# Turning the second batch's attention weights and the last normalised tiles by DMA, after splitting them into halves

## The reference

```python
def _layernorm(x, axis=-1, eps=1e-05):
    m = jnp.mean(x, axis=axis, keepdims=True)
    v = jnp.var(x, axis=axis, keepdims=True)
    return (x - m) / jnp.sqrt(v + eps)
...
        Q = jnp.einsum('btx,dx->btd', text, Wq) + bq
        K = jnp.einsum('bpx,dx->bpd', features, Wk) + bk
...
        scores = jnp.einsum('btd,bpd->btp', Q, K) * scale
        attn = jax.nn.softmax(scores, axis=-1)
        attended = jnp.einsum('btp,bpd->btd', attn, features)
...
        gate = _matmul_lora(x, gate_w, gate_a, gate_b)
        up = _matmul_lora(x, up_w, up_a, up_b)
        hidden = jax.nn.silu(gate) * up
        out = _matmul_lora(hidden, down_w, down_a, down_b)
```

## Time and profile before

| | us |
|---|---|
| median of 3 executions | 1181.67 |
| lowest and highest | 1180.48, 1183.46 |
| the profiled execution, its time | 1183.68 |
| the profiled execution, its span | 1181.9 |
| mean granted TensorE clock | 0.991 |

### The profile page before, as it was taken

How to read it: one execution, slowest core, us unless ns; L and a number is a source line. 1 busy time by engine, 2 the same in 40 slices (tenths; PEclk the granted TensorE clock), 3 DMA queues, 4 the chain that set the end, 5 groups by cost and what they waited for, 6 DMA issues and landing times.

```text
span 1181.9 us, 16528 instructions
## 1 busy us (share of the span) xinstructions
PE 1124.5 (95%) x6416; PEld 564.7 (48%) x6422; DVE 787.8 (67%) x1571; ACT 482.3 (41%) x723; POOL 166.0 (14%) x194
## 2 busy tenths in 40 slices
PE   4786999899989999999999999999999999999998
PEld 2353554744445444555444444444444444444444
DVE  8999988889994187977767676676766662222220
ACT  6896753772144224535343443434343341111110
POOL 4883340082004010210000000000000000000000
PEclk9997999999999999999999999999999999999999
DMA  9620000123032034201211212121211421111310
GB/s 370 262 93 1 2 1 1 72 80 100 1 107 86 1 94 157 107 1 38 71 58 50 72 36 72 37 72 36 72 50 30 150 66 48 48 48 49 126 47 18
DMA packets 25919, 83.58 MB, mean 71 GB/s; under 512 B 3633, under 2 KB 4273, under 8 KB 25841
## 3 DMA queue, kind: packets, MB, share of 16 engines
q1 hardware_dynamic: 25840, 82.53, 20.3%
HBM read 76.22 MB, written 6.29 MB: 70 GB/s over the span
## 4 chain that ended last, share of the span: by engine, by line
PE 72%; DVE 19%; ACT 5%; issue 2%; DMA 1%; SPq 0%; ACTq 0%; DVEq 0%
PE PAIR L2380 32%; PE PAIR L2019 11%; PE PAIR L2020 11%; PE PAIR L2021 11%; DVE X L1449 2%; PE PAIR L2337 1%; DVE BST L1247 1%; DVE BST L1248 1%; DVE PAIR L1401 1%; DVE POOL L1275 1%; PE PAIR L2412 1%; DVE LORA L1400 1%; DVE X L1318 1%; DVE LORA L1402 1%; DVE XT L1312 1%
## 5 line engine op out<-in xcount | busy, mean ns | idle before, releaser
L2019 PE MATMUL PAIR<-POOL 128*128 128x512 f16 x672 | 255.8, 381 | 2.4 <-DVE POOL L1492 2.4
L2020 PE MATMUL PAIR<-POOL 128*128 128x512 f16 x672 | 255.6, 380 | 0.0
L2021 PE MATMUL PAIR<-POOL 128*128 128x512 f16 x672 | 255.6, 380 | 0.0
L2380 PE MATMUL PAIR<-XT,POOL 128*128 128x512 f16 x1008 | 228.2, 379 | 0.0
L2380 PEld LDWEIGHTS PAIR<-XT,POOL 128*128 128x128 f16 x1008 | 97.8, 98 | 113.7
L2380 PE MATMUL PAIR<-X,POOL 128*128 128x512 f16 x504 | 115.7, 379 | 0.0
L2021 PEld LDWEIGHTS PAIR<-POOL 128*128 128x128 f16 x672 | 65.8, 98 | 80.3 <-issue 1.4
L2019 PEld LDWEIGHTS PAIR<-POOL 128*128 128x128 f16 x672 | 65.6, 98 | 67.5 <-DVE POOL L1492 4.1
L2020 PEld LDWEIGHTS PAIR<-POOL 128*128 128x128 f16 x672 | 65.7, 98 | 63.8 <-issue 0.6
L1634 DVE SCALAR_TENSOR_TENSOR STG<-STG,PAIR 128x1024 f32<-128x1024 f32 (+2 forms) x32 | 28.3, 884 | 90.0 <-PE PAIR L2412 90.0
L952 ACT ACTIVATE POOL<-STG 128x1024 f16<-128x1024 f32 (+2 forms) x32 | 25.3, 790 | 148.1 <-DVE STG L1634 148.1
(11 more groups left out here) (306 smaller groups left out, 1758.1 us busy)
## 6 DMA issues: line engine op xcount, KB each, us to landing
STG<-in_gate_w SPq DMA_DIRECT2D x21, 512.0 KB, 3.6
STG<-in_up_w SPq DMA_DIRECT2D x21, 512.0 KB, 4.3
STG<-in_ctx_t SPq DMA_DIRECT2D x16, 512.0 KB, 4.0
STG<-in_ctx SPq DMA_DIRECT2D x16, 512.0 KB, 4.3
STG<-in_down_w SPq DMA_DIRECT2D x16, 512.0 KB, 3.5
POOL<-in_ctx SPq DMA_DIRECT2D x12, 512.0 KB, 11.2
X<-in_x SPq DMA_DIRECT2D x8, 512.0 KB, 9.8
out_t<-X SPq DMA_DIRECT2D x16, 256.0 KB, 2.9
```

Of the source, the lines that this page charges most:

```text
L2019: e.matmul(dst, l_hi, r_hi, start=first, stop=False)
L2020: e.matmul(dst, l_hi, r_lo, start=False, stop=False)
L2021: return e.matmul(dst, l_lo, r_hi, start=False, stop=last)
L2380: i = e.matmul(dst, blk[:, a_, k, :], src[:, b_, k, :], start=(opens and k == 0 and n == 0), stop=(k == KD // 2 - 1 and n == 2), skip_grou ...
```

## The change

No transpose of these tiles is left on PE. The float32 value is first split where it lies, in rows, and the two float16 halves are turned by DMA transposes that SP issues.

- Weights of tiles 4 to 7: `weights_hi` and `weights_lo` split Y[1] into TURN[0] (in XT); `turn_weights(g)` issues two DMA transposes of 128x1024 into AT. `attend(g)` waits for them on x_in[g].
- H4[0..3]: split into TURN[1], `turn_fourth(u)` issues two of 128x1024 each.
- The five pieces of each t: `difference(t, p)`, now all 16 on DVE (T2's goes into PSUM), `piece_hi` on ACT and `piece_lo` on DVE, 20 of each, and `turn_piece(t, p)`, two DMA transposes of 128x512 each, 40 in all. Source space is short, so for t = 1 ACT waits ahead of B22 and DVE ahead of the low half of T2 until all ten transposes of t = 0 have landed; `keep_first(j)` waits for those of t = j.
- PE's S1(0) waits for all pieces of t = 0 and 1 and T1 of t = 2 and 3; S2(0), S4(0), S3(0) and A22(0) for T2, B22, T3 and T4 of t = 2 and 3.
- SP's list gets the 56 transposes: those of tiles 4 and 5 between context loads, those of tiles 6 and 7 and of H4[0..3] after the first four weight loads, the 40 pieces after the spill and the next two loads. All stand on the one SP queue.

```diff
+TURNED = 48
+T1, T2, B22, T3, T4 = range(5)
+LANDED = 32
...
+def turn_order(t, p):
+
+    return 5 * t + p if t < 2 else 10 + 2 * p + t - 2
...
+        TURN = [[XT[:, b, :, :, :].rearrange("p s k t -> p (s k t)")[:, 2 * D * t:2 * D * (t + 1)]
+                 .rearrange("p (s n) -> p s n", s=2) for t in range(BT)] for b in range(B)]
...
+        def wait_turned(e, t, p=None):
+
+            if t < 2:
+                e.wait_ge(turn_in(t, p), LANDED + 5 * 32)
+            else:
+                e.wait_ge(turn_in(t, p), LANDED + 2 * 32)
+
+        def difference(e, t, p):
 
             b11, b21, b12, b22 = (H4[g][:, h * HALF:(h + 1) * HALF] for g in (t, BT + t) for h in range(2))
...
+            if p == T1:
+                e.wait_ge(n4_ok, BT + t + 1)
+                e.wait_ge(x4t_lo, t + 1)
+                e.tensor_tensor(b11, b12, b11, ALU.subtract).then_inc(tg_ok, 1)
...
+            def turn_weights(g):
+                t = g % BT
+                e.wait_ge(at_lo, g + 1)
+                e.wait_ge(av_p, t + 1)
+                for s_ in range(2):
+                    e.dma_start_transpose(AT[:, s_, :, t * P:(t + 1) * P], TURN[0][t][:, s_, :]).then_inc(x_in[g], 16)
+
+            def turn_fourth(u):
+                for g in range(BT, NT):
+                    e.wait_ge(x_in[g], TURNED)
+                e.wait_ge(x4t_lo, u + 1)
+                for s_ in range(2):
+                    e.dma_start_transpose(XT[:, 0, s_, :, u * P:(u + 1) * P], TURN[1][u][:, s_, :]).then_inc(x_in[u], 16)
+
+            def turn_piece(t, p):
+                if t == 0 and p == T1:
+                    for u in range(BT):
+                        e.wait_ge(x_in[u], TURNED)
+                    e.wait_ge(spilled, 16 * BT)
+                e.wait_ge(x4t_lo, BT + turn_order(t, p) + 1)
+                e.dma_start_transpose(placed(t, p)[:, 0], high_half(t, p)).then_inc(turn_in(t, p), 16)
+                e.dma_start_transpose(placed(t, p)[:, 1], low_half(t, p)).then_inc(turn_in(t, p), 16)
...
+            def piece_lo(t, p):
+                e.wait_ge(x4t_hi, BT + turn_order(t, p) + 1)
...
+                elif t == 1 and p == T2:
+                    wait_turned(e, 0)
+                e.tensor_tensor(low_half(t, p), value(t, p), high_half(t, p), ALU.subtract).then_inc(x4t_lo, 1)
...
@@ -1913,44 +2009,60 @@
             slab_add(3)
             add_attended(4)
             stats_of(4)
+            norm_ask(4, 5)
             fourth_lo(0)
             fourth_lo(1)
-            attended_terms(4)
+            norm_rest(4, 5)
+            fourth_lo(2)
+            fourth_lo(3)
             block_lo(0, "S3")
             block_lo(0, "A22")
+            add_attended(5)
+            stats_of(5)
+            norm_ask(5, 6)
+            for p in (T1, T2, T3):
+                difference(e, 0, p)
+            norm_rest(5, 6)
+            piece_lo(0, T1)
+            difference(e, 0, T4)
+            for p in (T2, B22, T3, T4):
+                piece_lo(0, p)
             form(1, "S1")
             block_lo(1, "A11")
             block_lo(1, "A12")
...
             add_attended(6)
             stats_of(6)
             norm_ask(6, 7)
...
+            for p in (T1, T2, T3):
+                difference(e, 1, p)
             norm_rest(6, 7)
...
+            piece_lo(1, T1)
+            difference(e, 1, T4)
+            for p in (T2, B22, T3, T4):
+                piece_lo(1, p)
             add_attended(7)
             stats_of(7)
             norm_ask(7, 8)
...
+            difference(e, 2, T1)
+            difference(e, 2, T2)
             norm_rest(7, 8)
...
             gate_first(0)
...
+            piece_lo(2, T1)
+            block_lo(1, "S1")
+            difference(e, 3, T1)
+            difference(e, 3, T2)
+            piece_lo(3, T1)
```

## The result

| | before | after |
|---|---|---|
| median of 4 runs each, us | 1182.57 (1180.48 to 1183.70) | 1192.55 (1191.65 to 1195.27) |
| profiled execution: time, span, us | 1183.68, 1181.9 | 1192.47, 1190.7 |
| mean granted clock of TensorE | 0.99 | 0.979 |

A forecast was written before the change was run, and what follows sets the result against it. PE was taken to bound the stage, DVE next: 15.6 us of transposes, 4.0 idle and some 1.3 of small gaps, less 6.5, 3.4 and 0.9, gave 10.1; less 1.1 for the clock, 9: 1172.7 us, range 1168 to 1212 (own 1168 to 1178).

The forecast's parts named there:

- r: Time one transposed half piece (128 KB) occupies the DMA queue, taken as 0.35 us; no row showed a DMA transpose.
- break-even of 0.94: Time per half piece, in us, at which A22(0) starts so late that the whole gain is spent.
- The wide half: A half of a 1024-wide tile on the DMA queue, taken as twice a half piece, 0.7 us to issue.
- rival 1: DMA queue becomes the bound at about 1.2 us per half piece: A22(0) 14.6 us late, around 1196; chance 27 in 100.
- the sum: Added-up engine and queue times of the stage up to S1(1), giving a stage gain of 10.1 us.
- the queue to run empty: Once, because DVE must see t = 0 landed before its pieces of t = 1: some 4 us.
- its own signs: A12(0) late because DVE waits at a `piece_lo` for a DMA; gaps of even length ahead of S2, S4, S3, A22.
- Work off PE: 144 transposes leave PE, 15.6 us, with idle times before them; A11(0) could begin at 505.0, 15.3 us earlier.
- DVE as the bound: DVE late ahead of A12(0) loses 6.5 us, ahead of S1(0) 3.4, ahead of A22(0) 0.9.
- The gain of 9 us: Whole kernel: stage gain of 10.1 us less 1.1 for the clock, median 1172.7; chance 44 in 100.
- The weights' 3.5 us: PE time of the 32 weight transposes, part of the 144 transposes counted at 15.6 us.
- The clock: Lower PE clock behind the 6.5 and 3.4 us gaps: 1.1 us lost in all, between 0 and 3.4.

The follow-up runs named there:

- e1: The changed kernel with the 20 low halves of the pieces not turned, products reading the high halves twice: 1173.0 us, 0.9913 of the kernel before.
- the paired kernel: The changed kernel with piece halves laid side by side, turned by 20 DMAs of 1024 columns instead of 40, some splits earlier: 1176.0 us, 0.9944 of before.
- e4: The changed kernel with piece halves turned in pairs, 20 DMAs instead of 40, without DVE's wait for t = 0: 1176.0 us, 0.9944 of before.
- e3: The kernel before with only the weights of tiles 4 to 7 turned by 8 wide DMAs, H4 and pieces left on TensorE: 1181.3 us, 0.9994 of before.

## Why the prediction was wrong, point by point

- **The term that failed is r**, the time of one half piece. It was taken as 0.35 us, from the row of a plain DMA, since such rows "stand nearest to it in kind". It measured 1.31, above the break-even of 0.94. The step behind it, that such a DMA would be issued like a plain one and overlap with the next, is what failed: SP is held for 1.2 us by each. The other row of the same group, 1.2 us for backed-up issues, is nearer in number, but a transpose is at that price without a queue in front of it: in e1 one was issued at 516.89, 5.1 us behind the one before and with a DMA share of 0.00 from 515 to 517 us, and took 1.19 us. Wide ones took 1.23 behind a pause of SP (in the paired kernel). Neither of the two rows was a measurement of this kind of DMA, and a row of a plain DMA says nothing about a transposing one.
- **The wide half was taken as 2r**; it measured 1.47, not 2.6. The chain closes with the measured prices: SP begins H4 at 482.0; the eight wide halves take 11.8, where rival 1 at its 1.2 us for r has 19.2; spill, loads and the wait for the spill to land take 7.4, to 501.3, where the sum has 3.6 (the rows it names show 5.4 from the spill to the end of the two loads, and the wait for the landing is missing); the start of the last piece comes 52.4 later (39 x 1.31, 0.5 of pause and 1.0 more in one issue of 2.3), where rival 1 has 48.0 and 4 for the queue to run empty, which it never did for more than 0.5; landing 2.5: 556.2, and A22(0) started at 556.4. That rival 1's 14.6 us came out as near as 11.3 is partly luck: 7.4 and 4 us too many stand against 3.8 and 4.4 too few.
- **Rival 1 is what happened**, by its own signs: A12(0) late because DVE waited at a `piece_lo` for a DMA, and further gaps ahead of S1(0), S2(0), S4(0) and A22(0), 4.7, 0.9, 3.5 and 1.6 us. One sign was off: S3(0) had none, and they were not even.
- **Work off PE: right.** By the mark at 315.03, A11(0) came 15.5 us earlier (205.3 us behind it before, 189.8 in the traces after and e1); 15.3 was forecast.
- **DVE as the bound: right as a mechanism.** In e1, where the queue doesn't bind, the gap ahead of A12(0) was 7.6 us against 6.5, of which 2.3 were DVE's wait for t = 0; that ahead of S1(0) was 1.8 against 3.4. In e4, without that wait, they were 7.4 and 3.8; DVE waited 0.7 us for ACT there twice, which the sum does not have. (The sum's own terms for DVE from 482.7 on give about 490 and not 491.1; by the mark the next `add_attended` came at 490.6.) A22(0) waited 0.4 against 0.9.
- **The gain of 9 us:** e1 measured 9 (1173.0 against 1182.0), the forecast 1172.7. That they meet so closely is luck. Its stage gained 7.4 us by the mark instead of 10.1 (9 with the clock's 1.1), and the other 1.6 lie ahead of the mark. So the sum of the stage was right to 1.6 us where its condition, a queue that doesn't bind, nearly held.
- **The weights' 3.5 us are worth nothing alone** (e3). The sum added PE's transposes as if each were worth its time. A11(0) shows that this holds for all of them together; e3 shows that it does not for a part.
- **The clock.** Granted 0.50 at 519 to 521, right behind the 14.3 us gap; 36 matmuls took 10.19 us where they take about 7.9 at full clock, S1(0) 4.39 and S4(0) 5.28 where 2.75 is usual: 6.4 us together, where 0 to 3.4 were allowed for. This is most of why PE is busy for only 8.0 us less, though 15.6 us of transposes left it. It costs little time in the kernel after, since the queue's prices alone give A22(0)'s start.

## What to carry to other kernels

Before work goes to a DMA queue in many small parts, find what one issue of that very kind costs, for a row of another kind gives no price; if no run has it, measure it by itself before the rewrite. Where an issue has a fixed price, fill it: here twice the columns in half as many DMAs turned 10 us lost into 6 us won, together with the splits that could then move. And ask of the largest gap whether it is the cause or only where the time is spent: splitting up a 14 us gap won nothing, while leaving out 20 of the DMAs, which no engine's busy time showed as costly, won 20 us.

## What the runs showed of the hardware

- A DMA that transposes 16-bit data inside SBUF, issued from SP, mostly costs 1.19 to 1.27 us of SP at 128x512, the 1.19 with nothing else under way (e1, at 516.89); a plain DMA was issued in 0.33 us. At 128x1024 it is 1.23 behind a pause and 1.34 behind another (1.38 to 1.47 from start to start), at 128x2048 1.32 with none ahead of it and 2.65 from start to start.
- The DMA engines' busy share was 0.50 with narrow ones one behind another and 0.95 with wide ones, at 100 and 178 GB/s. Landing took 2.5 us for 512 columns and 3.3 to 3.5 for 1024 (H4 and pieces), at the median.
- TensorE's matmuls at 0.95 DMA share from transposes ran as before: 0.216 us from one to the next and 12.0 us busy of 12 (482 to 494 us).
- One POOL subtraction of 128x512 in f32 held a 0.16 us DVE instruction for 1.03 us, to its own end.
